# Linear attention with decay on one Trainium2 core: the scores of two slots made together, and the first half of the state's update moved next to a slot's values

## The reference, cut to what matters

```
q, k = elu(x @ Wq) + 1, elu(x @ Wk) + 1        # 16 heads of 64
v    = x @ Wv
a    = sigmoid(x @ Wa + ba + 2)                # one decay per token and head
step:  S = a * S + k (outer) v ;  z = a * z + k
out    = (q . S) / (q . z + 1e-6)
x      = x + out @ Wo
```

## Time and profile before

| | us |
|---|---|
| three timed runs | 1111.17, 1111.70, 1115.77 (median 1111.7) |
| the profiled execution | 1113.79 |
| its span in the trace | 1112.0 |
| TensorE busy in it | 996.2 (90%) |
| VectorE, ScalarE, GpSimd busy | 749.8, 749.5, 438.5 |
| mean granted TensorE clock | 0.953 of full |

### The profile page before, as it was taken

The page is one execution under the profiler, slowest core; times in us unless marked ns, Lnnn a source line. Parts: engine busy times, 40 slices in busy tenths (PEclk is TensorE's granted clock), DMA queues, the critical chain, the costliest instruction groups (busy, mean ns, idle before and its releaser), DMA issues. The chain is left out here.

```text
span 1112.0 us, 27303 instructions
## 1 busy us (share of the span) xinstructions
PE 996.2 (90%) x10432; PEld 673.2 (61%) x10432; DVE 749.8 (67%) x1513; ACT 749.5 (67%) x1513; POOL 438.5 (39%) x580
## 2 busy tenths in 40 slices
PE   5889999999999999848999889999999999589993
PEld 3333333333333334537999757877777777479993
DVE  6789999999999998883333355666666666533333
ACT  4658888888888887535666476676767676446663
POOL 3742112221112222225775215545445445257751
PEclk9889999999999999987999889999999999679997
DMA  2234111111111100422111321202111110111114
GB/s 72 86 104 123 35 30 33 45 44 30 31 31 33 47 13 2 165 74 62 50 48 44 117 107 54 78 39 78 42 75 48 68 67 12 39 39 47 48 42 128
DMA packets 40038, 64.73 MB, mean 58 GB/s; under 512 B 10024, under 2 KB 21032, under 8 KB 37992
## 3 DMA queue, kind: packets, MB, share of 16 engines
q1 hardware_dynamic: 31736, 50.14, 14.1%
q0 software_dynamic: 4992, 10.23, 3.5%
q10 hardware_dynamic: 3184, 2.63, 0.8%
HBM read 47.86 MB, written 14.68 MB: 56 GB/s over the span
## 5 line engine op out<-in xcount | busy, mean ns | idle before, releaser
L802 ACT ACTIVATE PB<-S 128x512 f32<-128x512 f32 x576 | 307.9, 597 | 71.1 <-PE S L608 66.2
L908 DVE TENSOR_REDUCE mx<-S 128x2 f32<-128x1024 f32 (+1 forms) x192 | 207.5, 1127 | 8.5 <-PE S L594 8.5
L870 POOL TENSOR_SCALAR_AFFINE_SELECT PB<-PB 128x512 f32<-128x512 f32 x128 | 79.3, 638 | 306.4 <-ACT PB L802 306.3
L643 PE MATMUL PV<-PB,VP 128*32 128x256 f32 (+2 forms) x2432 | 177.7, 379 | 0.0
L1526 DVE TENSOR_TENSOR m_hs<-m_gs,m_UP 128x512 f32<-128x512 f32 x78 | 53.6, 688 | 159.3 <-ACT m_gs L1362 157.2
L608 PE MATMUL S<-W 50*128 50x512 bf16 (+3 forms) x768 | 123.9, 328 | 4.9 <-ACT PB L802 4.2
L594 PE MATMUL S<-W 48*128 48x512 bf16 (+3 forms) x640 | 94.4, 326 | 13.1 <-DVE mx L904 4.9
L1202 POOL DMA_INDIRECT yd_rows<-m_ys,m_target x78 | 76.8, 984 | 59.5 <-DVE m_ys L1533 59.5
L1196 POOL DMA_INDIRECT m_xs<-xn_rows,m_source x78 | 76.0, 974 | 45.4 <-issue 23.2
L643 PEld LDWEIGHTS PV<-PB,VP 128*32 128x32 f32 x2432 | 51.6, 108 | 69.1 <-issue 59.4
L594 PEld LDWEIGHTS S<-W 48*128 48x128 bf16 x640 | 26.8, 94 | 108.4 <-issue 43.1
(11 more groups left out here) (315 smaller groups left out, 1920.9 us busy)
## 6 DMA issues: line engine op xcount, KB each, us to landing
d_LQ<-l_rows SPq DMA_DIRECT2D x15, 1024.0 KB, 4.7
W<-qk_parts SPq DMA_DIRECT2D x210, 32.0 KB
qk_parts<-OT SPq DMA_DIRECT2D x24, 256.0 KB, 3.0
W<-qk_parts SPq DMA_DIRECT2D x30, 96.0 KB
W<-in_L_ffn_w_gate SPq DMA_DIRECT2D x1, 2048.0 KB, 9.3
W<-in_L_ffn_w_up SPq DMA_DIRECT2D x1, 2048.0 KB, 14.4
xn_rows<-m_XN SPq DMA_DIRECT2D x8, 256.0 KB, 2.3
m_GB<-yd_rows SPq DMA_DIRECT2D x8, 256.0 KB, 6.4
```

Source lines behind the costliest of these rows:

```text
L643: ins = nc.tensor.matmul(PV[32 * u:32 * u + 32, shift + col:shift + end], VP[:, g, kb, u // 2, :], PB[:, slot, col:end], start=(kb == 0 an ...
L802: nc.scalar.activation(PB[:, j % NPB, :], S2[:, j % 3, :], ACT.Exp, scale=SC).then_inc(exp_done, 1)
L870: nc.gpsimd.affine_select(out=tri, in_=tri, compare_op=ALU.is_ge, fill=0.0, base=0, pattern=[[0, U], [1, P]], channel_multiplier=-1).then_ ...
L908: nc.vector.reduce_max(mx[:, g % 2, c, :, heads[0], qb], S1[:, b, :, 0:w], AX.X)\
```

## The change

The function `scores` now makes two slots (c = 0: slots 0 and 1, c = 1: slots 2 and 3) in one go, 8 matmuls, the even slot into columns 0 to 255 of both banks and the odd slot into columns 256 to 511. It is called twice in a step in place of four times: after slot 1 for slots 2 and 3, and after slot 3 for slots 0 and 1 of the next step. `state(t, b, 0)` goes ahead of the scores in slot 1. VectorE's `weigh` reads the half that its slot has, and waits for the scores of both slots of the pair.

```diff
-                def scores(t, b, i):
-
-                    if i or from_(t, 1):
-                        pe.wait_ge(w_done, t * 4 + i)
-                    if i % 2 == 0:
-                        pe.wait_ge(kt_copied, t * 2 + (1 + i // 2))
-                        pe.wait_ge(elu_done, t * 4 + (3 + i // 2))
-
-                    for r in range(2):
-                        for a in range(2):
-                            q = slice(64 * a, 64 * a + 64)
-                            last = nc.tensor.matmul(AT[:, a, r * P:(r + 1) * P], KT[q, b, 2 * i + r], QT[q, b, 2 * i + r],
-                                                    start=True, stop=True)
-                    last.then_inc(at_done, 1)
+                def scores(t, b, c):
+
+                    if c or from_(t, 1):
+                        pe.wait_ge(w_done, t * 4 + 2 * c)
+                    pe.wait_ge(kt_copied, t * 2 + (1 + c))
+                    pe.wait_ge(elu_done, t * 4 + (3 + c))
+                    for i in (2 * c, 2 * c + 1):
+                        for r in range(2):
+                            for a in range(2):
+                                q = slice(64 * a, 64 * a + 64)
+                                col = (2 * (i % 2) + r) * P
+                                last = nc.tensor.matmul(AT[:, a, col:col + P], KT[q, b, 2 * i + r], QT[q, b, 2 * i + r],
+                                                        start=True, stop=True)
+                        last.then_inc(at_done, 1)
 
                 def slot(t, b, i, last=False):
                     across_chunks(t, b, i)
                     within_chunk(t, b, i)
-                    if i < 3:
-                        scores(t, b, i + 1)
-                    elif not last:
+                    if i == 1:
+                        state(t, b, 0)
+                        scores(t, b, 1)
+                    elif i == 3 and not last:
                         scores(t + 1, 1 - b, 0)
 
                 def step(t, b, last=False):
                     slot(t, b, 1)
-                    state(t, b, 0)
                     for c in range(2):
 
                 def weigh(t, i):
                     dve.wait_ge(masked, t * 4 + (i + 1))
-                    dve.wait_ge(at_done, t * 4 + (i + 1))
+                    dve.wait_ge(at_done, t * 4 + 2 * (i // 2) + 2)
                     if i >= 2 or from_(t, 1):
                         dve.wait_ge(intra_done, t * 4 + (i - 1))
-                    nc.vector.tensor_tensor(WB[:, i % 2].rearrange("p a r n -> p a (r n)"), AT[:, :, 0:2 * P],
+                    nc.vector.tensor_tensor(WB[:, i % 2].rearrange("p a r n -> p a (r n)"),
+                                            AT[:, :, (i % 2) * 2 * P:(i % 2 + 1) * 2 * P],
                                             DM[:, i].rearrange("p a r n -> p a (r n)"), ALU.mult).then_inc(w_done, 1)
```

## The result

| | before | after |
|---|---|---|
| timed runs, median (range) | 1112.99 (1111.17 to 1115.77), 4 | 1097.75 (1096.88 to 1100.53), 4 |
| ratio, 95% interval | | 0.9873 (0.9848 to 0.9897) |
| span of the profiled execution | 1112.0 | 1098.8 |
| slot 0 of step 1 to slot 0 of step 15 | 255.2 | 239.8 |

The kernel became 15.2 us faster at the median; the forecast was 14.9. In two later groups of runs the same kernel gave ratios of 0.9845 (0.9805 to 0.9885) and 0.9853 (0.9820 to 0.9886). So the direction is certain, and the three intervals together span 1.0 to 2.0%. That the median came within 0.3 us of the forecast is in part luck: the first interval reaches from 11 to 17 us. What bears the argument is the loop.

The account below looks back on a forecast made before the run. The prediction took TensorE's own sequence plus one wait a step as the bound. Terms of 14 x -1.08 = -15.1, -0.34 and +0.5 gave -14.9, so 1111.7 - 14.9 = 1096.8 us, range 1093.7 to 1102.

Parts of the forecast that it names:

- The bound: Decay loop: set by TensorE's own sequence, 18.23 us a step, plus one late arrival a step in slot 0.
- The ends of blocks: TensorE, slots 0 to 3: two scores visits and two OI ends saved, -0.69 us a step.
- both seams: OI next to SU, and the middle of the double scores block: each taken to cost 0 us.
- the first rival: Seams of OI and SU pay a weight load: 0.28 us a step stays, 1100.7 us in all; chance 0.12.
- The wait: Slot 0: TensorE's wait for VectorE's weighted scores is filled by the double scores block, -0.39 us a step.
- The other slacks: Waits of weigh, state and turned keys in a full step: all stay hidden, with 0.27 to 1.6 us to spare.
- The slack before the state: Slot 1: state(t, 0) waits for the other half's update, with 0.74 us to spare.
- The irregular 1.4 us: Loop's 14 steps: 255.25 us less 14 plain steps of 18.13 leaves 1.4 us of irregular moments, let stand.
- Step 15, +0.5: Last step: state(15, 0) waits for the late update with the double scores behind it, turned outputs 0.5 us later.
- Step 0, -0.34: Slot 1 waits for weights behind a GpSimd mask, so slot 0's -0.79 is lost; +0.30 and -0.64 remain.
- The last projection, 0: After the loop: 3.96 us at clock 0.50 against 2.12 at 1.00; change bounded by 1.84 either way, taken as 0.
- The sum: Whole kernel: 14 x -1.08 = -15.1, -0.34 and +0.5 make -14.9 us, a median of 1096.8 us.

Follow-up runs that it names:

- Five kernels with other sequences: Changed kernel: state(t, 0) behind scores, 241.94; slots 2, 3 paired only, 250.30; slots 0, 1 only, 242.58. Kernel before: state moved alone, 253.08; slot 3's scores twice, 255.84.
- extra scores: Changed kernel with slot 0's four score matmuls made twice in slot 3's double block: 14 steps 244.94 us, ratio to the kernel before 0.9894.
- the update late by 1.80: Changed kernel with three unused VectorE instructions ahead of the update of the state's second half: 14 steps 256.87 us, ratio to the kernel before 1.0054.

## Why the prediction was right, point by point

- **The bound.** TensorE's sequence plus one wait a step: right. Five kernels with other sequences came out within 0.4 us of the block sums over 14 steps (241.9, 253.1, 250.3, 242.6, 255.8 for 241.8, 253.2, 250.4, 242.9, 255.9). Two sums were further off: 244.9 for 246.0 (extra scores, three waits left out) and 256.9 for 253 to 255 (the update late by 1.80, its cover taken too large).
- **The ends of blocks, -0.69 a step.** Right; the measured blocks are 1.09 and 1.09 in place of 1.09 and 1.08. The value taken for both seams, 0, is what the rows show. The rule on weight loads that made the first rival, from the Trainium skill ("TensorE: Matmul & The Clock Gate", Part 3), doesn't hold at this seam: SU's loads start at 926.86 in step 15, while OI's matmuls run from 926.40 to 927.09. SU's first record starts 0.52 after OI's first, and 8 pairs at 0.06 are 0.48. What is left, 0.05, is OI's own slow first pair, which the sum left out there and had inside SU's 0.61; the two cancel. The Trainium skill ("TensorEngine Tiling (Array Packing)", Key Properties) says that a change of the tiling mode drains the array, and a change of tile alone doesn't. These rows agree in the cost: 0.20 us for a visit of the 64-row shape, and nothing at a seam of one shape; the draining itself no row shows. The prediction says that nothing in the trace shows OI next to SU. But the trace of the kernel before did have other seams of one shape, turned keys next to queries on the whole array:

```profile
823.59 1.06 PE L1714 MATMUL d_PA<-d_xc,d_WQ 128*128 128x128 f32 x8
824.49 0.61 PE L1730 MATMUL d_TR<-ident,d_Kn 128*128 128x128 f32 x4
824.94 1.06 PE L1714 MATMUL d_PA<-d_xc,d_WQ 128*128 128x128 f32 x8
```

Eight records take 0.90 here and four take 0.45, that is 0.11 each and nothing for the seam. The first turned keys of the step, which stand behind a scores block, take 0.49 (823.10 to 823.59). These rows spoke for 0 at the seam of OI and SU, and weaken the first rival.
- **The wait, -0.39 a step.** Right, and shown from both sides by the added matmuls: 0.05 a step in the kernel before, 0.45 in the changed one. It goes wholly in 11 of the 14 steps. The three behind a marking of experts waited 0.44 longer than the others before, and still wait 0.38.
- **The other slacks.** None turned into a wait in a full step. The slack before the state, put at 0.74, measured 0.63: in the changed kernel TensorE is there 3.96 after slot 0's values and the update ends at 3.19, but 0.15 passes between the update's end and the first matmul that waited for it (929.59 to 929.74).
- **The irregular 1.4 us** were left to stand, and unexplained. They are the marking of experts: the steps from 5 to 6, 9 to 10 and 13 to 14 take 18.57 where a plain one takes 18.13, which makes 1.3, and in the changed kernel 17.43 against 17.05. So these three steps gain 1.14 each, and the 14 steps 15.4 and not 14 x 1.08 = 15.1. A look at VectorE's timeline in steps 5, 9 and 13 would have found them.
- **Step 15, +0.5.** Right in its mechanism; it measured 0.65. The update ends 3.19 after slot 0's values in both kernels, as assumed; what the sum left out is the 0.15 between its end and SU's start.
- **Step 0, -0.34.** It measured -0.27. From slot 0's values in step 0 to those in step 1 it was 16.96 before (668.05 to 685.01), and 16.69 in all three profiles of the changed kernel, at a granted clock of 1.00.
- **The last projection, 0.** Its 16 records took 3.96 before, and 3.51, 2.09 and 3.48 in the three profiles of the changed kernel, at a granted clock of 0.59, 1.00 and 0.59. The bound of 1.8 was of the right size, but it isn't the loop's length that decides: one kernel shows both ends of it.
- **The sum.** The terms measured add up to -15.38 - 0.27 + 0.65 = -15.0 against -14.9 forecast. The median gave -15.2. In the two profiled executions it is only 13.2, and the loop isn't the reason: the stretch ahead of the first projection of keys, whose code is unchanged, was 2.6 longer (653.8 to 656.4), and from there to slot 0's values of step 0 it was 0.8 shorter (14.26 to 13.44), in a stretch where the granted clock was 0.81 before and 0.87 after. The larger part of the spread thus lies ahead of the loop, and the forecast had no term for it.

## What to carry to other kernels

Where TensorE is the bound with small matmuls, count what lies between the blocks: list the starts of blocks, subtract the pace within a block, and what remains is paid per change of shape and can be taken away by putting blocks of one shape side by side. Move the freed or gathered work to where TensorE waits for a chain that it can't shorten; the same matmuls cost 0.05 us there and 0.45 elsewhere. Then check each wait that now has more behind it, above all in the last step, where the work that used to stand in between is missing.

## What the runs showed of the hardware

A visit of four score matmuls of 64 x 128 costs 0.20 us beyond the 0.11 for each pair; the OI block of 128 x 64 costs 0.14 beyond its 0.06 per pair. Two such blocks with different PSUM buffers and two semaphore waits between them run on as one. That a seam with waits costs nothing that the trace can show, when they are long satisfied, was not obvious beforehand. A wait that isn't satisfied adds some 0.15 us between the end of VectorE's update and the first matmul that waited for it (929.59 to 929.74 in step 15).

The loop repeats to 0.02 us in 240 over three executions of one kernel, at a granted clock of 1.00. The part ahead of it doesn't: with the same code it took 651.9 to 658.5 us in the profiles here. Two of the changed kernel (length, busy by engine, granted clock):

```profile
0.00:656.44 656.44, 586.98 (x6185) 326.89 (x6186) 504.20 (x882) 459.50 (x870) 210.33 (x280) 0.95 0.20 58
...
0.00:651.90 651.90, 581.08 (x6186) 321.18 (x6186) 504.09 (x882) 459.29 (x870) 210.83 (x280) 0.97 0.20 58
```

The other engines' busy times are the same; TensorE's differs by 5.9 and the mean granted clock is 0.95 against 0.97, that is, more of the longer one passed at the 1.2 GHz level. This is the spread of the timed runs, and a change of 2 us has to be read in the trace, not in them.
